# A hybrid transformer block on one core: the plan of all stages with TensorE's measured durations, a set duration for changes of its tile shape, and a small weight on a stage's age

## The chip, the core and the metric

One core of a Trainium2 chip runs the whole program: TensorE (PE, with its weight loads PEld), VectorE (DVE), ScalarE (ACT), GpSimd (POOL), SyncE (SP, which here only issues DMAs) and the core's 16 DMA engines. The metric is the device time in microseconds (us) of one execution, the median over runs. One further execution was taken by the hardware profiler, and all rows in this document come from it.

## The reference, cut to what matters

x has 8 batches of 512 tokens, width 128, in fp32. Four residual sublayers follow each other, each behind a layer norm:

```python
x = x + attn_a(layernorm(x))   # 16 heads, q and k of 8 + 32 features, softmax, v of 8, Wo, all with biases
x = x + ffn(layernorm(x))      # top-1 of 8 experts: silu(x W1 + b1) W2 + b2, hidden width 512, times the gate
x = x + attn_b(layernorm(x))   # differential: 16 heads, softmax(q1 k1) - lam * softmax(q2 k2), v of 16, W_proj
x = x + ffn(layernorm(x))      # the same experts and gate again
```

## The kernel before, in words

**Groups.** The attention work is cut into 96 groups of four heads of one batch. Groups 0 to 31 are attention a (four groups a batch), groups 32 to 95 attention b (eight groups a batch, four for each of the two softmaxes). The program counts 16 "batches" b: 0 to 7 in attention a, 8 to 15 in attention b. In this document *stage A* is the program up to group 31 and *stage B* the part from group 32 to the last group.

**What one group costs.** TensorE computes every score twice. `smax` (L1131) gives 16 pieces of 128 x 512, one for each of four query tiles and four heads; VectorE reduces each to row maxima in `rowmax` (L1479). The maxima are turned (`mrow`, L1137), copied by ScalarE and sent by DMA into an extra row of the stacked operand STK. `score` (L1152) then gives 16 transposed pieces with the maximum already subtracted; ScalarE takes the exponent (`expo`, L1355) into P, and `pv` (L1165, four times a group) multiplies by V. ScalarE copies the result (`ocopy`, L1362), TensorE turns it (`oturn`, L1173) and VectorE divides (`normal`).

**The rest.** For each batch there are the turned input (`hturn`, L1087), the feature tiles (`feat`, L1099: six a batch in stage A, four in stage B), the values (`vproj`, L1107 to L1115), the turned and projected output (`aturn` L1182, `oproj` L1193/L1199), the gate (`gturn`, `glogit`, `gplace`), and 92 expert blocks of 128 rows (`xturn` L1238, `up` L1246, `down` L1261). In stage B the features pass through GpSimd (`turned`, `b_lo`) and DMAs (`put`, `stack`) before a group can use them. The last 19 expert blocks run behind the last group.

**Three tile shapes.** In stage A `smax` and `score` use 120 or 121 rows of the array. In stage B they use 32 rows each, in the strip of their head j (rows 32j to 32j+31), so that up to four run side by side; these are called *row tiles* here. `pv` writes 32 columns each for four heads side by side (*column tiles*). Everything else uses the whole array. A *visit* is an unbroken run of row tiles, between two stages of another shape.

**PSUM.** Of the eight banks one is `pv`'s; the other seven go round among all other stages. `smax` may hold four, `score` three. `smax` and `score` ask for one bank or two neighbouring ones; VectorE and ScalarE read two banks with one instruction if they come as a pair.

**What sets the order.** All engines run in program order, and that order is written out by `schedule()` (L192), a list scheduler that plays the whole program at build time. `STAGES` holds an engine and a duration for each stage, `HOP` the time until another engine sees the end, `LANDS` that of a DMA. Every job asks for its next stage with a *rank*, its age in units of groups (`smax` of group g has g - 1.92, the feature tiles of a batch are spread over the groups before it is needed). The inner loop (L667) takes, over all engines, the request with the earliest start, and among equal starts the lowest rank:

```python
key = (start, rank)
if best is None or key < best[0]:
    best = (key, e, k)
```

For TensorE there is a `rows_free` time for each of the four row strips. In the plan of before a row tile in stage B occupies the engine for 0.03 us and its strip for 0.22, and a change of shape costs nothing by itself; the durations of the whole and column stages stand for what they take on average (`pv` 1.02, `up` 1.1, `gplace` 0.5).

Of the kernel before, what the change touches and what calls it, by code (L numbers as in the profile page):

```python
# [16 lines left out]
B = 8  # L17
# [142 lines left out]
def ends_of_segment(k):  # L160
# [3 lines left out]


STAGES = {
    "smax": ("tensor", 0.216), "score": ("tensor", 0.216), "pv": ("tensor", 1.02), "mrow": ("tensor", 0.11), "oturn": ("tensor", 0.45),
    "hturn": ("tensor", 0.45), "feat": ("tensor", 0.86), "vproj": ("tensor", 1.0), "aturn": ("tensor", 0.45), "oproj": ("tensor", 1.3), "gturn": ("tensor", 0.45), "glogit": ("tensor", 0.8),
    "gplace": ("tensor", 0.5), "xturn": ("tensor", 0.11), "up": ("tensor", 1.1), "down": ("tensor", 1.1),
    "rowmax": ("vector", 1.13), "normal": ("vector", 0.6), "join": ("gpsimd", 0.8), "split": ("gpsimd", 1.6), "ln_stats": ("vector", 1.3),  # L170
    "ln_apply": ("gpsimd", 2.4), "ln_apply_q": ("vector", 1.45), "columns": ("vector", 3.0), "flo": ("vector", 0.63),
    "resid": ("vector", 0.68),
# [5 lines left out]
    "gate_exp": ("scalar", 0.25), "silu_z": ("scalar", 0.48), "weigh": ("scalar", 0.2), "plus_p": ("gpsimd", 0.5), "mix": ("vector", 1.4), "wsum": ("tensor", 0.95), "silu_t": ("scalar", 0.49), "lambda_exp": ("scalar", 0.25),  # L178
    "index": ("gpsimd", 0.4), "ln_rstd": ("gpsimd", 0.6), "turned": ("gpsimd", 8.4), "silu_p": ("gpsimd", 2.8), "b_lo": ("gpsimd", 2.7), "scatter": ("gpsimd", 4.1), "send": ("gpsimd", 1.1),
    "xload": ("sync", 0.6), "setup": ("sync", 0.6), "put": ("sync", 1.8), "stack": ("sync", 1.2), "mput": ("sync", 0.6), "weights": ("sync", 1.1),  # L180
    "rows": ("sync", 1.1), "blank": ("sync", 0.6), "fill": ("sync", 9.0), "weights_b": ("sync", 0.6), "weights_p": ("sync", 0.6),
    "wload": ("sync", 1.0), "wstore": ("sync", 0.6),
}
HOP = {"tensor": 0.23, "vector": 0.13, "scalar": 0.14, "gpsimd": 0.15, "sync": 0.05}
LANDS = {"xload": 4.0, "setup": 3.0, "put": 3.0, "stack": 3.0, "mput": 2.0, "weights": 5.0, "rows": 3.8, "blank": 6.0, "weights_b": 4.0,
         "weights_p": 3.0, "wload": 14.0, "wstore": 8.0, "scatter": 4.0, "fill": 5.0, "send": 4.0}
FROM = [(19.77, 0.35), (33.0, 0.5), (74.0, 0.6), (100.00, 0.10)]

MAIN = ("smax", "rowmax", "score", "expo", "pv")
ENGINES = ("tensor", "vector", "scalar", "gpsimd", "sync")  # L190
# [2 lines left out]
def schedule(ticks=False):  # L193


    clock = {"tensor": 0.0, "vector": 3.5, "scalar": 3.0, "gpsimd": 5.0, "sync": 1.8}
    order = {e: [] for e in ENGINES}
    ended, ring, marks = {}, {}, []

    rows_free = [0.0] * 4  # L200
    idle = {bank: 0.0 for bank in RB}
    holder = {bank: None for bank in RB}
    asked, blocked = {e: [] for e in ENGINES}, {}
# [6 lines left out]
        yield from behind(stage, index)  # L210
        yield ("do", rank, stage, index, 0, us, engine)

    def fill_bank(rank, stage, *index):
        yield from behind(stage, index)
        yield ("do", rank, stage, index, 1, None, None)

    def fill_pair(rank, stage, *index):

# [13 lines left out]
    def find_banks(n, t, stage):  # L232

        kind = stage if stage in MOST else "other"
        held = sum(1 for bank in RB if bank not in idle and (holder[bank][0] if holder[bank][0] in MOST else "other") == kind)
        if held >= MOST[kind]:
            return None
        pair, single = free_banks(2) if n == 2 and held + 2 <= MOST[kind] else None, free_banks(1)
        if single is None:
            return None  # L240
        if n == 2 and held > 1 and kind == "smax":
            return pair
        return pair if pair and pair[0] <= max(t, single[0]) else single

    def rows_of(stage, index, n):
        if stage in ("smax", "score") and index[0] >= 4 * B:
            return range(index[-1] % 4, index[-1] % 4 + n)
        return range(4)
# [196 lines left out]
    def values_of(b, rank):  # L445
        if b in (0, 1, 2, B, B + 1, B + 2):
            if b >= 3:
                yield from after(("pv", (end_of(b - 3), 3)))
            yield from do(rank, "columns", b, us=3.0 if b < 3 else 0.4)
        if b >= 3:  # L450
            yield from after(("pv", (end_of(b - 3), 3)))
        if b == 0:
            yield from after(("setup", (3,)))
        for c in range(1 if b < B else 2):
            yield from fill_bank(rank, "vproj", b, c)
            yield from do(rank, "vcopy", b, c)
            give("vproj", b, c)

# [26 lines left out]
    def batch_ends():  # L485
        for b in range(NB):
            rank = first_of(b + 1) + (0.5 if closes(b) else 1.73)
# [6 lines left out]
                give("aturn", b, c)  # L494
            if b >= B:
                yield from after(("weights_p", ()))
            yield from fill_bank(rank, "oproj", b)
            yield from do(rank, "resid", b)
            give("oproj", b)
            rank += 0.2  # L500
# [23 lines left out]
            if closes(b):  # L524
                k = seg_of(b)
# [13 lines left out]
    def rank_of(m):  # L539
        k, i = BLOCKS[m]  # L540
        return FROM[k][0] + FROM[k][1] * i

# [125 lines left out]
    while any(asked.values()):  # L668
        best = None
        for e in ENGINES:  # L670
            for k, (rank, t, job, stage, index, bank, us) in enumerate(asked[e]):
                if bank:
                    found = find_banks(bank, max(t, clock[e]), stage)
                    if found is None:
                        continue
                    t = max(t, found[0])
                start = max(t, clock[e])
                if e == "tensor":
                    start = max([start] + [rows_free[r] for r in rows_of(stage, index, found[2] if bank else 1)])
                key = (start, rank)  # L680
                if best is None or key < best[0]:
                    best = (key, e, k)
        if best is None:
            raise RuntimeError("no stage can be placed")
        (start, _), e, k = best
        rank, t, job, stage, index, bank, us = asked[e].pop(k)
        if bank:
            _, first, n = find_banks(bank, max(t, clock[e]), stage)
            if stage in ("smax", "score"):
                us = n * (us if index[0] < 4 * B else 0.03)  # L690
            ring[stage, index] = [(b, holder[b]) for b in range(first, first + n)]
            for b in range(first, first + n):
                del idle[b]
                holder[b] = (stage, index)
        clock[e] = start + us
        more = 0.0
        if e == "tensor":
            taken = rows_of(stage, index, len(ring.get((stage, index), [0])))
# [5 lines left out]
        end = start + us + more + LANDS.get(stage, HOP[e])  # L704
# [1135 lines left out]
```

## Time and profile before

| | us |
|---|---|
| median of 3 runs | 1573.26 |
| lowest, highest | 1565.8, 1590.58 |
| the profiled execution: span | 1602.4 |
| PE busy over the span | 1416.2 (88%) |
| DVE busy | 1181.5 (74%) |
| ACT busy | 1080.7 (67%) |
| POOL busy | 693.2 (43%) |

No time outside the span is recorded for the profiled execution, so its span stands for its time: it is 29.1 us above the median of the three runs and 11.8 above the slowest. A busy share is a mean over stages with different limits, matmuls overlap, and their ends are modelled; how long PE was really held by one stage is read from the start of that stage to the start of the next. In the chain of waits each piece is what held up the next one; shares of the chain tell which engine came last.

### The profile page before, as it was taken

How to read it: one execution, taken by the hardware profiler on the slowest of the kernel's cores; microseconds unless marked ns; L12 is line 12 of the kernel's file. 1: busy time of each engine (PE TensorE's matmuls, PEld its weight loads, DVE VectorE, ACT ScalarE, POOL GpSimd, SP SyncE). 2: the span in 40 equal slices, each digit the busy share in tenths (PEclk: the TensorE clock that was granted, in tenths of full speed). 3: DMA queues.
4: the chain of work that ended last, by engine and by line, in shares of the span. 5: the costliest groups of instructions: out<-in, count | busy, mean ns of one | idle time of the engine just before them, and what ended most of it. 6: DMA issues, size and time to landing. Idle time of an engine off the chain costs nothing.

```text
span 1602.4 us, 26934 instructions
## 1 busy us (share of the span) xinstructions
PE 1416.2 (88%) x9196; PEld 597.4 (37%) x9196; DVE 1181.5 (74%) x2011; ACT 1080.7 (67%) x1787; POOL 693.2 (43%) x758
## 2 busy tenths in 40 slices
PE   3999999999999997889998899888888998998656
PEld 1334333345554332445433223222232544442245
DVE  4777788776767788647787887888787787779333
ACT  1566666766556776758786787787776886887612
POOL 3412334233414755666646581342511846552123
PEclk7999999999999999979999998999997998999868
DMA  6677676956742255978211220201205642411034
GB/s 189 187 232 229 187 237 175 264 164 194 210 117 77 78 177 165 300 206 231 84 30 40 61 60 21 80 27 41 57 24 187 194 120 91 132 39 34 1 123 136
DMA packets 131005, 208.46 MB, mean 130 GB/s; under 512 B 16611, under 2 KB 96128, under 8 KB 130870
## 3 DMA queue, kind: packets, MB, share of 16 engines
q1 hardware_dynamic: 121560, 192.40, 41.0%
q0 software_dynamic: 6016, 12.71, 2.3%
q10 hardware_dynamic: 3294, 1.64, 0.4%
q8 instruction: 74, 1.21, 0.3%
q14 instruction: 61, 0.50, 0.1%
HBM read 127.33 MB, written 80.77 MB: 130 GB/s over the span
## 4 chain that ended last, share of the span: by engine, by line
PE 65%; DVE 12%; ACT 6%; POOL 6%; issue 4%; DMA 4%; SPq 2%; ACTq 0%; another core or an unknown queue 0%; POOLq 0%; DVEq 0%
PE ps L1165 19%; PE ps L1131 12%; PE ps L1152 11%; DVE Mb L1479 7%; PE ps L1261 5%; PE ps L1246 5%; ACT P L1355 4%; PE ps L1099 4%; POOL ROW L1423 3%; PE ps L1173 2%; POOL rs L1701 1%; PE ps L1199 1%; PE ps L1218 1%; DVE st L1447 1%; DMA STK<-qka 1%
## 5 line engine op out<-in xcount | busy, mean ns | idle before, releaser
L1479 DVE TENSOR_REDUCE Mb<-ps 128x2 f32<-128x1024 f32 (+1 forms) x957 | 939.6, 1008 | 255.6 <-PE ps L1131 245.9
L1355 ACT ACTIVATE P<-ps 128x512 f32<-128x512 f32 (+1 forms) x1077 | 804.1, 780 | 250.4 <-PE ps L1152 232.0
L1131 PE MATMUL ps<-STK 32*128 32x512 f16 (+1 forms) x1536 | 418.1, 394 | 46.9 <-DMA STK<-qka 18.2
L1152 PE MATMUL ps<-STK 32*128 32x512 f16 (+1 forms) x1536 | 417.0, 392 | 40.9 <-ACT P L1355 25.0
L1165 PE MATMUL ps<-P,V 128*32 128x512 f32 x3072 | 425.7, 627 | 6.5 <-ACT P L1355 5.9
L1131 PEld LDWEIGHTS ps<-STK 32*128 32x128 f16 (+1 forms) x1536 | 103.1, 94 | 290.6 <-issue 109.4
L1152 PEld LDWEIGHTS ps<-STK 32*128 32x128 f16 (+1 forms) x1536 | 106.1, 93 | 268.9 <-issue 77.6
L1746 POOL DMA_INDIRECT xs<-ROW,slot x64 | 63.6, 993 | 136.3 <-DVE slot L1569 121.1
L1753 POOL TENSOR_TENSOR TH<-TH,Z 128x512 f32<-128x512 f32 x54 | 68.6, 1270 | 91.6 <-ACT Z L1403 91.1
L1165 PEld LDWEIGHTS ps<-P,V 128*32 128x32 f32 x3072 | 61.3, 109 | 124.4 <-issue 102.1
L1246 PE MATMUL ps<-XT,WE 128*128 128x128 f32 x696 | 102.3, 294 | 1.9 <-ACT XT L1385 1.1
L1246 PEld LDWEIGHTS ps<-XT,WE 128*128 128x128 f32 x696 | 89.4, 200 | 27.9 <-issue 13.4
L1710 POOL CAST HL<-RT 128x512 f16<-128x512 f32 x42 | 25.7, 613 | 151.2 <-ACT RT L1294 140.9
L1261 PEld LDWEIGHTS ps<-WE,Z 128*128 128x128 f32 x584 | 74.2, 199 | 36.4 <-issue 18.9
L1261 PE MATMUL ps<-WE,Z 128*128 128x128 f32 x584 | 86.0, 292 | 1.6 <-ACT P L1355 0.8
L1099 PE MATMUL ps<-HT,WA 128*128 128x512 f32 x160 | 86.2, 641 | 1.2 <-ACT HT L1280 0.8
L1768 POOL DMA_INDIRECT x<-X x46 | 46.4, 1009 | 81.4 <-DVE X L1651 65.6
L1699 POOL TENSOR_SCALAR vs<-mv 128x4 f32<-128x4 f32 x32 | 7.5, 234 | 167.2 <-DVE mv L1450 167.2
L1423 POOL TENSOR_SCALAR ROW<-ROW,mv,rs 128x128 f32<-128x128 f32 x100 | 78.4, 793 | 2.4
L1362 ACT COPY OR<-ps 128x512 f32<-128x512 f32 x96 | 56.4, 588 | 23.4 <-PE ps L1165 22.0
L1755 POOL TENSOR_TENSOR Z<-Z,TH 128x512 f32<-128x512 f32 x54 | 68.6, 1271 | 4.2
L1737 POOL TENSOR_TENSOR AT<-AT,OT 128x256 f32<-128x256 f32 x32 | 23.3, 728 | 108.4 <-DVE OT L1501 108.3
(156 smaller groups left out, 1407.0 us busy)
## 6 DMA issues: line engine op xcount, KB each, us to landing
WE<-wx SPq DMA_DIRECT2D x87, 576.0 KB
STK<-qka SPq DMA_DIRECT2D x62, 480.0 KB
qka<-HL SPq DMA_DIRECT2D x96, 256.0 KB
STK<-qkb SPq DMA_DIRECT2D x64, 256.0 KB
xs<-pad SPq DMA_DIRECT2D x8, 1554.0 KB
qkb<-HL SPq DMA_DIRECT2D x96, 128.0 KB
X<-xs SPq DMA_DIRECT2D x73, 129.5 KB, 3.7
qka<-HL SPq DMA_DIRECT2D x48, 128.0 KB
```

Of the source, the lines that this page charges most:

```text
L1099: eng.matmul(ps[:, bank, :], WA[:, 128 * x:128 * x + 128], HT[:, b % 2, :], start=True, stop=True).then_inc(sem("pr"), 1)
L1131: mm = eng.matmul(ps[:, bank + i, :], l_, r_, start=True, stop=True)
L1152: mm = eng.matmul(ps[:, bank + i, :], l_, r_, start=True, stop=True)
L1165: mm = eng.matmul(ps[32 * j:32 * j + 32, OB, :], V[:, b % 3, kt, vw * h:vw * h + 32], P[:, st % 3, j, :], start=(kt == 0), stop=(kt == 3))
L1246: mm = eng.matmul(ps[:, bank, 128 * c:128 * c + 128], w_[:, 128 * c:128 * c + 128], xt_, start=True, stop=True)
L1261: mm = eng.matmul(ps[:, bank, 0:128], z[:, 128 * c:128 * c + 128], w_[:, FH + D * c:FH + D * c + D], start=(c == 0), stop=(c == 3))
L1355: eng.activation(P[:, st % 3, j:j + n, :], ps[:, bank:bank + n, :], ACT.Exp, scale=SCALE_A if g < 4 * B else SCALE_B).then_inc(sem("exp"), 1)
L1423: eng.tensor_scalar(ROW[:, t0 + i, 0:128], ROW[:, t0 + i, 128:256], mv[:, z, i, 0:1], rs[:, z, i:i + 1], ALU.subtract, ALU.mult).then_inc( ...
L1479: eng.tensor_reduce(Mb[:, g % 2, at:at + 4 * n - 3:4], ps[:, bank:bank + n, :], AX, ALU.max).then_inc(sem("mx"), 1)
L1746: eng.indirect_dma_start(out=xs[k][:, :], out_offset=bass.IndirectOffsetOnAxis(ap=slot[:, t:t + 1], axis=0), in_=ROW[:, t, 0:ROWW], in_off ...
L1753: eng.tensor_tensor(th, th, z, ALU.mult).then_inc(sem("fq"), 1)
L1755: eng.tensor_tensor(z, z, th, ALU.add).then_inc(sem("fsp"), 1)
```

## The change

Nothing that is computed changes, and no instruction gets another shape except that a pair of pieces can become two singles and the reverse. The planner gets other numbers and two new rules:

- tensor durations: the middle lines of the diff, and `vproj` and `oproj` of stage B get durations of their own (0.87, 1.78);
- `TURN = 0.097`: a stage of another shape than the one before it starts at the earliest 0.097 after the work on all four strips has ended;
- a row tile holds its strip for its full 0.216 a piece, and the engine's own clock moves on by 0.01;
- `WEIGHT["tensor"] = 0.08`: among the requests on TensorE the one with the smallest start + 0.08 x rank is taken. Across the engines the earliest start still decides.

```diff
-    "smax": ("tensor", 0.216), "score": ("tensor", 0.216), "pv": ("tensor", 1.02), "mrow": ("tensor", 0.11), "oturn": ("tensor", 0.45),
+    "smax": ("tensor", 0.216), "score": ("tensor", 0.216), "pv": ("tensor", 0.88), "mrow": ("tensor", 0.11), "oturn": ("tensor", 0.44),
...
-    "gplace": ("tensor", 0.5), "xturn": ("tensor", 0.11), "up": ("tensor", 1.1), "down": ("tensor", 1.1),
+    "gplace": ("tensor", 0.21), "xturn": ("tensor", 0.11), "up": ("tensor", 0.89), "down": ("tensor", 0.89),
...
-HOP = {"tensor": 0.23, "vector": 0.13, "scalar": 0.14, "gpsimd": 0.15, "sync": 0.05}
+TURN = 0.097
+HOP = {"tensor": 0.21, "vector": 0.13, "scalar": 0.14, "gpsimd": 0.15, "sync": 0.05}
...
+WEIGHT = {"tensor": 0.08, "vector": 0.0, "scalar": 0.0, "gpsimd": 0.0, "sync": 0.0}
...
+    def shape_of(stage, index):
+
+        if stage in ("smax", "score") and index[0] >= 4 * B:
+            return "rows"
+        return "columns" if stage == "pv" else "whole"
...
                 if e == "tensor":
-                    start = max([start] + [rows_free[r] for r in rows_of(stage, index, found[2] if bank else 1)])
-                key = (start, rank)
-                if best is None or key < best[0]:
-                    best = (key, e, k)
+                    if shape_of(stage, index) == shape[0]:
+                        start = max([start] + [rows_free[r] for r in rows_of(stage, index, found[2] if bank else 1)])
+                    else:
+                        start = max([start] + [free + TURN for free in rows_free])
+                key = (start + WEIGHT[e] * rank, rank)
+                if mine is None or key < mine[0]:
+                    mine = (key, (start, rank), e, k)
+            if mine and (best is None or mine[1] < best[0]):
+                best = mine[1:]
...
-            if stage in ("smax", "score"):
-                us = n * (us if index[0] < 4 * B else 0.03)
+            if stage in ("smax", "score") and index[0] < 4 * B:
+                us = n * us
...
-            more = 0.19 if len(taken) < 4 else 0.0
-            for r in taken:
-                rows_free[r] = start + us + more
+            shape[0] = shape_of(stage, index)
+            for r in rows_of(stage, index, len(ring.get((stage, index), [0]))):
+                rows_free[r] = start + us
+            if shape[0] == "rows":
+                clock[e] = start + 0.01
```

Counted over TensorE's whole order, what the new plan does to it is this (a change of shape is a stage whose shape differs from that of the stage ahead of it):

| | before | after |
|---|---|---|
| changes of shape, stage A | 240 | 238 |
| changes of shape, stage B | 1077 | 915 |
| visits in stage B | 490 | 423 |
| `smax` pairs and singles, stage B | 374, 276 | 358, 308 |
| `score` pairs and singles, stage B | 284, 485 | 257, 540 |
| order of TensorE behind the last group | 64 stages | the same 64 |

**Place 1**, TensorE, in group 80, where experts run. Two `pv` (L1165, in the new file L1180) of one group and what stands ahead of each. L1131 and L1152 are `smax` and `score` (now L1146 and L1167), L1261 `down` (now L1276), L1246 `up` (now L1261). The array shape is not in these rows: all on STK are row tiles here. Before:

```order
L1131 MATMUL ps<-STK 128x512 x2
L1152 MATMUL ps<-STK 128x512
L1261 MATMUL ps<-WE,Z 128x128 x4
L1152 MATMUL ps<-STK 128x512 x2
L1131 MATMUL ps<-STK 128x512
L1165 MATMUL ps<-P,V 32x512 x4
L1131 MATMUL ps<-STK 128x512 x2
L1152 MATMUL ps<-STK 128x512 x2
L1246 MATMUL ps<-XT,WE 128x128 x4
L1131 MATMUL ps<-STK 128x512 x2
L1152 MATMUL ps<-STK 128x512 x2
L1165 MATMUL ps<-P,V 32x512 x4
```

The same group with the change (L1197 `aturn`, L1253 `xturn`, L1114 a feature tile of batch 15, L1214 `oproj`):

```order
L1146 MATMUL ps<-STK 128x512 x2
L1167 MATMUL ps<-STK 128x512
L1276 MATMUL ps<-WE,Z 128x128 x4
L1197 MATMUL ps<-idf,AT 128x128 x4
L1253 MATMUL ps<-idf,X 128x128
L1114 MATMUL ps<-HT,WA 128x512
L1214 MATMUL ps<-WA,ATT 128x128 x8
L1261 MATMUL ps<-XT,WE 128x128 x4
L1167 MATMUL ps<-STK 128x512 x2
L1146 MATMUL ps<-STK 128x512
L1180 MATMUL ps<-P,V 32x512 x4
```

Before, each whole stage stood alone between two visits; now six of them stand in one block, with one change of shape into it and one out of it.

**Place 2**, TensorE, in group 68, where no expert runs: one stretch between two `pv`. Before, with a feature tile of batch 15 (L1099) between two visits:

```order
L1165 MATMUL ps<-P,V 32x512 x4
L1131 MATMUL ps<-STK 128x512 x2
L1152 MATMUL ps<-STK 128x512 x2
L1099 MATMUL ps<-HT,WA 128x512
L1131 MATMUL ps<-STK 128x512 x2
L1152 MATMUL ps<-STK 128x512 x2
L1131 MATMUL ps<-STK 128x512 x2
L1165 MATMUL ps<-P,V 32x512 x4
```

The same stretch with the change:

```order
L1180 MATMUL ps<-P,V 32x512 x4
L1146 MATMUL ps<-STK 128x512 x2
L1167 MATMUL ps<-STK 128x512
L1146 MATMUL ps<-STK 128x512
L1167 MATMUL ps<-STK 128x512 x2
L1180 MATMUL ps<-P,V 32x512 x4
```

The feature tile has gone to a later place (batch 15's four tiles stood at groups 68 to 69 and stand at 73 to 80 now; those of batches 10, 12, 13 and 14 are moved and spread alike), and the visit holds six pieces where two visits held four and six.

## Rows read from the trace of the kernel before

**Rows 1.** Busy time by stage: engine, busy us (instructions), then PEclk, DMA share, GB/s.
```profile
37.00:555.00 518.00, 496.88 (x2861) 211.82 (x2861) 396.66 (x689) 333.53 (x500) 193.28 (x222) 1.00 0.63 184
555.00:1508.00 953.00, 855.84 (x5940) 332.06 (x5938) 737.21 (x1159) 721.39 (x1236) 461.19 (x475) 0.95 0.34 101
1508.00:1602.00 94.00, 53.37 (x376) 48.49 (x372) 33.38 (x109) 19.24 (x43) 24.86 (x26) 0.76 0.35 111
```

**Rows 2.** Chain of waits, 960 to 1230: share of that stretch by line.
```profile
by line: PE ps L1165 26.4%; DVE Mb L1479 12.0%; PE ps L1152 10.8%; PE ps L1131 9.8%; ACT P L1355 9.6%; issue 5.4%; POOL ROW L1423 4.6%; PE ps L1099 3.2%; PE ps L1173 2.8%; PE ps L1199 2.2%; PE ps L1115 2.0%; POOL rs L1701 1.5%; PE ps L1218 
```

**Rows 3.** Chain of waits, 1230 to 1508: share by line.
```profile
by line: PE ps L1165 26.0%; PE ps L1131 11.9%; PE ps L1152 10.8%; PE ps L1246 10.5%; ACT P L1355 10.0%; PE ps L1261 9.8%; DVE Mb L1479 3.9%; PE ps L1173 3.8%; issue 3.0%; DVE X L1638 2.1%; PE ps L1238 1.5%; PE ps L1199 1.4%; PE ps L1137 1.0
```

**Rows 4.** Waits, 555 to 1508: who for whom, us, times, longest.
```profile
DVE Mb L1479 <- PE ps L1131: 159.3, 212, 6.2
ACT P L1355 <- PE ps L1152: 122.6, 188, 3.2
```

**Rows 5.** Timeline of PE: start us, us to last modelled end, line, shapes, count.
```profile
1273.55 1.16 PE L1246 MATMUL ps<-XT,WE 128*128 128x128 f32 x8
1274.55 1.06 PE L1261 MATMUL ps<-WE,Z 128*128 128x128 f32 x8
1275.54 0.39 PE L1152 MATMUL ps<-STK 32*128 32x512 f16 x2
1275.55 0.39 PE L1131 MATMUL ps<-STK 32*128 32x512 f16 x1
1275.86 1.06 PE L1165 MATMUL ps<-P,V 128*32 128x512 f32 x8
...
1281.30 1.16 PE L1246 MATMUL ps<-XT,WE 128*128 128x128 f32 x8
1282.39 0.39 PE L1131 MATMUL ps<-STK 32*128 32x512 f16 x2
```

**Rows 6.** Chain of waits, 836 to 872: start us, us, what.
```profile
841.30 0.44 PE ps L1173 x4
...
852.28 1.86 PE ps L1165 x8
...
862.72 1.05 PE ps L1099 x2
...
864.09 1.00 PE ps L1165 x8
...
869.23 0.59 PE ps L1182 x4
```

**Rows 7.** Chain of waits, 0 to 90.
```profile
61.90 0.86 PE ps L1099 x2
```

**Rows 8.** Timeline of PE, 1084 to 1086: a visit of seven pieces.
```profile
1084.50 0.39 PE L1131 MATMUL ps<-STK 32*128 32x512 f16 x2
1084.51 0.60 PE L1152 MATMUL ps<-STK 32*128 32x512 f16 x4
1084.73 0.37 PE L1131 MATMUL ps<-STK 32*128 32x512 f16 x1
1085.98 0.66 PE L1173 MATMUL ps<-idf,OR 128*128 128x128 f32 x4 [0.88 <-ACT P L1355]
```

**Rows 9.** Groups by form, DVE, 555 to 1508: busy us, mean ns, idle before.
```profile
L1479 DVE TENSOR_REDUCE Mb<-ps 128x2 f32<-128x1024 f32 x375 | 452.2, 1220 | 129.3 <-PE ps L1131 124.4 <-remote 2.4 <-issue 0.6
L1479 DVE TENSOR_REDUCE Mb<-ps 128x1 f32<-128x512 f32 x276 | 184.3, 684 | 36.9 <-PE ps L1131 34.9 <-issue 0.3
```

**Rows 10.** Groups by form, ACT, 555 to 1508.
```profile
L1355 ACT ACTIVATE P<-ps 128x1024 f32<-128x1024 f32 x285 | 291.2, 1025 | 62.2 <-PE ps L1152 58.4 <-issue 0.8 <-ACT Mt L1333 0.6
L1355 ACT ACTIVATE P<-ps 128x512 f32<-128x512 f32 x485 | 277.7, 600 | 72.2 <-PE ps L1152 64.2 <-issue 3.8 <-remote 1.1
```

**Rows 11.** Windows, line L1165 alone: PE busy (matmuls), PEld busy, PEclk, DMA, GB/s.
```profile
1198.00:1226.00 28.00, 11.61 (x48) 1.21 (x48) 0.51 0.36 124
1226.00:1274.00 48.00, 12.79 (x96) 1.89 (x96) 1.00 0.73 223
```

More of the change, by code:

```diff
@@ L166 @@
 STAGES = {
-    "smax": ("tensor", 0.216), "score": ("tensor", 0.216), "pv": ("tensor", 1.02), "mrow": ("tensor", 0.11), "oturn": ("tensor", 0.45),
-    "hturn": ("tensor", 0.45), "feat": ("tensor", 0.86), "vproj": ("tensor", 1.0), "aturn": ("tensor", 0.45), "oproj": ("tensor", 1.3), "gturn": ("tensor", 0.45), "glogit": ("tensor", 0.8),
-    "gplace": ("tensor", 0.5), "xturn": ("tensor", 0.11), "up": ("tensor", 1.1), "down": ("tensor", 1.1),
+    "smax": ("tensor", 0.216), "score": ("tensor", 0.216), "pv": ("tensor", 0.88), "mrow": ("tensor", 0.11), "oturn": ("tensor", 0.44),
+    "hturn": ("tensor", 0.44), "feat": ("tensor", 0.86), "vproj": ("tensor", 1.1), "aturn": ("tensor", 0.44), "oproj": ("tensor", 1.1), "gturn": ("tensor", 0.44), "glogit": ("tensor", 0.92),
+    "gplace": ("tensor", 0.21), "xturn": ("tensor", 0.11), "up": ("tensor", 0.89), "down": ("tensor", 0.89),
     "rowmax": ("vector", 1.13), "normal": ("vector", 0.6), "join": ("gpsimd", 0.8), "split": ("gpsimd", 1.6), "ln_stats": ("vector", 1.3),
@@ L177 @@
     "vcopy": ("scalar", 0.5), "b_hi": ("scalar", 1.0), "acopy": ("scalar", 0.49), "gcopy": ("scalar", 0.49),
-    "gate_exp": ("scalar", 0.25), "silu_z": ("scalar", 0.48), "weigh": ("scalar", 0.2), "plus_p": ("gpsimd", 0.5), "mix": ("vector", 1.4), "wsum": ("tensor", 0.95), "silu_t": ("scalar", 0.49), "lambda_exp": ("scalar", 0.25),
+    "gate_exp": ("scalar", 0.25), "silu_z": ("scalar", 0.48), "weigh": ("scalar", 0.2), "plus_p": ("gpsimd", 0.5), "mix": ("vector", 1.4), "wsum": ("tensor", 0.86), "silu_t": ("scalar", 0.49), "lambda_exp": ("scalar", 0.25),
     "index": ("gpsimd", 0.4), "ln_rstd": ("gpsimd", 0.6), "turned": ("gpsimd", 8.4), "silu_p": ("gpsimd", 2.8), "b_lo": ("gpsimd", 2.7), "scatter": ("gpsimd", 4.1), "send": ("gpsimd", 1.1),
@@ L198, in schedule @@
     ended, ring, marks = {}, {}, []
-    rows_free = [0.0] * 4
+    rows_free, shape = [0.0] * 4, ["whole"]
     idle = {bank: 0.0 for bank in RB}
@@ L211, in do, with fill_bank @@
         yield ("do", rank, stage, index, 0, us, engine)
-    def fill_bank(rank, stage, *index):
+    def fill_bank(rank, stage, *index, us=None):
         yield from behind(stage, index)
-        yield ("do", rank, stage, index, 1, None, None)
+        yield ("do", rank, stage, index, 1, us, None)
     def fill_pair(rank, stage, *index):
@@ L454, in values_of @@
         for c in range(1 if b < B else 2):
-            yield from fill_bank(rank, "vproj", b, c)
+            yield from fill_bank(rank, "vproj", b, c, **({} if b < B else dict(us=0.87)))
             yield from do(rank, "vcopy", b, c)
@@ L496, in batch_ends @@
                 yield from after(("weights_p", ()))
-            yield from fill_bank(rank, "oproj", b)
+            yield from fill_bank(rank, "oproj", b, **({} if b < B else dict(us=1.78)))
             yield from do(rank, "resid", b)
@@ L670, in schedule @@
         for e in ENGINES:
+            mine = None
             for k, (rank, t, job, stage, index, bank, us) in enumerate(asked[e]):
@@ L694, in schedule @@
                 holder[b] = (stage, index)
-        clock[e] = start + us
-        more = 0.0
+        clock[e], hop = start + us, HOP[e]
         if e == "tensor":
-            taken = rows_of(stage, index, len(ring.get((stage, index), [0])))
-            more = 0.19 if len(taken) < 4 else 0.0
-            for r in taken:
-                rows_free[r] = start + us + more
+            shape[0] = shape_of(stage, index)
[3 more added lines that the diff above has]
+                clock[e] = start + 0.01
         order[e].append((stage, index))
         times[e].append((start, us, stage, index))
-        end = start + us + more + LANDS.get(stage, HOP[e])
+        end = start + us + LANDS.get(stage, hop)
         ended[stage, index] = end
```

## The prediction

> **What bounds the kernel now.** I read the busy time by stage first. In stage A TensorE is busy 496.88 of 518.00 us at full granted clock, in stage B 855.84 of 953.00 at a mean clock of 0.95, where VectorE has 737.21 (77%) and ScalarE 721.39 (76%) [rows 1]. Then the chain of waits: in the stretch without experts (960 to 1230) the lines of TensorE shown add up to 57.2%, with VectorE's reduce at 12.0% and the exponent at 9.6% [rows 2]; with experts (1230 to 1508) to 76.7%, the reduce at 3.9%, the exponent at 10.0% [rows 3]. The reader is to see that TensorE is what mostly comes last, and that stage B is not full on any engine: VectorE waited 159.3 us for `smax`, ScalarE 122.6 us for `score` [rows 4]. Seven PSUM banks go round between three engines, and whichever comes late hands its delay on. The 94 us behind the last group [rows 1] keep their order on TensorE.
>
> **The price of a change of shape.** I take starts. `up` at 1273.55 has row tiles before it and `down` behind it: 1.00 us to the next start. The `down`, with row tiles behind it: 0.99. The `up` at 1281.30 stands between row tiles on both sides: 1.09 [rows 5]. A feature tile among whole stages holds TensorE for 0.86 us [rows 7], between row tiles for 1.05 [rows 6]; four transposes for 0.44 and 0.59 [rows 6]. So one change costs 0.09 to 0.10 us; I use 0.10. The new TURN (0.097) is right, and durations without changes (0.86, 0.89, 0.44) are what the rows show once the changes are taken off. The Trainium skill, TensorEngine Tiling (Array Packing), Key Properties, says that changing the tiling mode drains TensorE, while changing only the tile does not. The trace agrees, with 0.10 us; the page has no price.
>
> **The sum, against the profiled 1602.4.**
>
> 1. Stage A: 240 changes become 238, the pieces are the same work, and an order on an engine that is busy 96% of the time cannot save more than its gaps, 21 us in all [rows 1]. I take 0, with 3 us either way.
> 2. Stage B, changes: 1077 - 915 = 162 fewer, 162 x 0.10 = 16.2 us less held by TensorE. TensorE is busy 90% of stage B [rows 1]; the chain gives it less, 57 to 77% [rows 2, 3]. An earlier end counts where TensorE is last, and I take the upper figure, because where it is not last the piece after next usually hangs on it again: 14.6. The lower end is 57%: 9.2.
> 3. Fuller visits: a visit with one piece a strip takes 0.32 us (1275.54 to 1275.86) [rows 5], and each further piece in the fullest strip about 0.22. Over all visits the pieces in the fullest strip add up to 714 before and 682 after: 32 x 0.22 = 7.0 us less at most. But a long visit waits for banks: the seven pieces from 1084.50 on took 1.48 us to the next start, 0.88 of it idle until the exponent gave a bank back [rows 8]. That row says that a longer visit saves nothing. I keep half, 3.5; ends 0 and 7.0.
> 4. Broken pairs: `smax` has 16 pairs fewer, `score` 27. Two singles cost VectorE 2 x 0.684 - 1.220 = 0.148 us more than a pair [rows 9], ScalarE 2 x 0.600 - 1.025 = 0.175 [rows 10]: 2.4 and 4.7 us. On the chain these two stand with some 4 to 12% and 10% each [rows 2, 3], but a single also gives its bank back earlier. I take 1.3 us of the 7.1; ends 0 and 7.1.
> 5. Long blocks. VectorE can hold four banks, two pairs, 2 x 1.22 = 2.44 us of work [rows 9]. If TensorE makes no visit for longer than that, VectorE must run dry, and ScalarE with its three banks earlier. With each stage at its duration without changes (0.90 for `pv`, that is 1.00 less one change; 0.86 for `feat`, 0.89 for `up` and `down`, 0.44 for four transposes, 0.11 for one, 0.87 for `vproj` and 1.78 for `oproj` as the new table has them) I find 2 such blocks in stage B before, 1.8 us over the limit together, and 21 after, 20.6 us over. Place 1 is the longest, 4.97 us. That is 18.8 us of new hunger on VectorE. Most of it falls where experts run, there the reduce is only 3.9% of the chain [rows 3] and VectorE has gaps to catch up in; I take a quarter, 4.7 us; ends 0 and 18.8.
> 6. Moved projections. The feature tiles of batches 10 and 12 to 15 come later, one every two groups instead of four close together. Their `put` stands at least two groups ahead of the first `stack` that wants it (batch 10: 42.25 against 44.75 in the new plan), and a group takes some 14 us (953 / 64 = 14.9), so the DMAs stay covered; if the cover of one batch went, its group would start late by up to a group's 15 us, once. POOL is busy 461.19 of 953 [rows 1] and takes batch 15's turning beside expert work. I take 0.
>
> Together: -14.6 - 3.5 + 1.3 + 4.7 = -12.1, so a like execution would span 1590.3. The change is taken as a number of us, since it stands on counts: 1573.3 - 12.1 = 1561.2. From the ends of the terms: -16.2 - 7.0 - 3 = -26 at one side, 1547; -9.2 + 7.1 + 18.8 + 3 = +20 at the other, 1593.
>
> **Rivals.**
>
> *More than the changes: the plan fits the chip.* The old plan gave `gplace` 0.5 us, where 0.21 stands now, and a row tile 0.03 us of the engine, and knew no change of shape, so its moments were wrong by tenths in each group. If the new order meets its partners on time, some of the 282 us that VectorE and ScalarE waited for TensorE [rows 4] goes, and spread feature tiles keep TensorE steadier where its clock fell. Half clock is dear: from 1198 to 1226 the granted clock was 0.51, the 1.2 GHz level, and six `pv` took 11.61 us busy there against twelve in 12.79 behind it [rows 11]; one held TensorE for 1.86 us instead of 1.00 [rows 6]. Six times 0.87 is 5.2 us, and I estimate another 4 for the visits around them: 9 of 28 us, a third. A mean clock of 0.95 means a tenth of stage B, 95 us, at half clock, which ties up some 31 us. If 15 of these came back and a tenth of half the waits, 14, the gain would be 12 + 15 + 14 = 41 us at best; half of the additions gives 1573.3 - 12.1 - 14.5 = 1547, the whole 1532. For it: every duration in the table is now what the rows show. Against: the waits are between engines that all work at 75% or more, and the old durations of `pv`, `up` and `down` already had the changes in them on average.
>
> *Evacuation sets the pace, and nothing comes of it.* The Trainium skill, TensorEngine Tiling (Array Packing), PSUM Bottleneck, warns that tiling speeds up TensorE and not the emptying of PSUM. As a mechanism here: what TensorE saves it spends waiting for a bank, as in the 0.88 us [rows 8], and the 3.5 and 14.6 are lost; left are the 1.3 of the singles: 1574.6. For it: VectorE and ScalarE wait on banks in the same ring, and the visits get longer. Against: these two themselves wait 282 us for TensorE, and TensorE's lines lead the chain [rows 2 to 4].
>
> *Long blocks starve the other two: slower.* The place is the stretches with experts and projections of stage B. The price is the whole 18.8 us of term 5 and the 7.1 of term 4. What gives it the decision is VectorE having no spare time to catch up in, that is from a busy share of it in those stretches near 90% on; then term 2 is worth its lower end: -9.2 + 18.8 + 7.1 = +17, 1590. If TensorE's clock then fell for half as long again in stage B, a further 15 us, 1605. For it: place 1 has 5 us without one row tile. Against: VectorE is at 77%, and experts also occupy TensorE longest.
>
> *The change does not do what it says* would be an order on the chip with other counts; the order is fixed in the program, so I give it no share.
>
> **How the numbers follow.** The forecast, 1561, has 0.5; the better fit, 1532 to 1547, 0.22; no gain, 1575, 0.18; slower, 1590 to 1605, 0.10. About 2% is what a measurement of this kernel can tell from no change: 1541.8 and 1604.7. Faster by over 2% is most of the better fit, half of its band and its tail, and a rest of the forecast: 0.20. Slower by over 2% needs the starving and the clock together: 0.04. Within 2%: 0.76. The range leaves out the far end of both: 1534 to 1588.
>
> **What would show it.** Right: stage A of the same length within 5 us; TensorE busy in stage B down by some 15 to 20 us with the same pieces; `up` and `down` in neighbouring pairs at 0.89 to 1.00; the exponent and reduce with a higher mean share of singles; waits of VectorE for `smax` about equal, with new single waits of 1 to 3 us behind blocks like place 1. Wrong: VectorE's waits for TensorE in stage B above 180 us (starving), or below 130 (fit); a mean granted clock in stage B away from 0.95 by more than 0.02; new waits of `smax` for `stack` DMAs near groups 48, 64, 72, 80 or 88 (term 6); stage A shorter by more than 5 us.

## The result, and the profile after

The changed kernel took 1561.86 us (median of 9 runs, 1554.73 to 1567.92) beside 1573.6 for the kernel before (also of 9): ratio 0.9922, 95% interval 0.9897 to 0.9948, or 12 us less. I had said 1561. In a second set of runs the ratio was 0.9839 (0.9773 to 0.9904). The size was right; how it comes about was in good part not what I wrote.

The profiled execution spans 1553.0 us. The one of before spanned 1602.4, more than any timed run of it, so the 49 us between them are not the change. I took a second profile of before (`before_again`), which spans 1586.0, and later one of the changed kernel (`after_again`), 1569.6: between the second profiles there are 16 us. By stage, the changed kernel (columns as in [rows 1]):

```profile
37.00:551.00 514.00, 497.02 (x2860) 212.83 (x2864) 393.72 (x696) 333.15 (x522) 192.04 (x220) 0.99 0.62 185
551.00:1462.00 911.00, 822.38 (x5943) 328.04 (x5940) 736.35 (x1176) 719.14 (x1264) 462.96 (x477) 0.98 0.36 106
1462.00:1553.00 91.00, 51.54 (x376) 46.99 (x372) 32.38 (x109) 19.91 (x43) 24.74 (x26) 0.75 0.35 114
```

and stage B of the second profile of before:

```profile
554.00:1491.00 937.00, 840.42 (x5944) 327.88 (x5940) 737.22 (x1159) 720.95 (x1237) 461.30 (x475) 0.97 0.35 103
```

Against the second profile of before, stage A is 3 us shorter, the tail 4, stage B 26 us at the same work of VectorE and ScalarE. TensorE is busy 18 us less in it, near the 16 counted, but only 9 less (831.77) in the changed kernel's second profile, whose stage B takes 926 us. The waits of the two, stage B of the changed kernel first, then of before, answer to [rows 4]:

```profile
DVE Mb L1494 <- PE ps L1146: 101.7, 146, 6.3
ACT P L1370 <- PE ps L1167: 79.5, 152, 2.0
```

```profile
DVE Mb L1479 <- PE ps L1131: 143.8, 209, 6.7
ACT P L1355 <- PE ps L1152: 116.2, 177, 3.2
```

79 us of waiting for TensorE have gone, and what is left of VectorE's, 101.7 (104.6 in the second profile), is below the 130 us that I had set as the sign of another cause. The other sign, a mean granted clock in stage B more than 0.02 from 0.95, is there in the first profile (0.98) and not in the second (0.97); the second profile of before has 0.97 as well. The place tells more. I cut stage B where the last `pv` of groups 31, 47, 71 and 95 starts: experts, none, experts. Columns as in [rows 1]. Before (second profile), then the changed kernel, then the last two stretches of the changed kernel's second profile:

```profile
583.00:845.00 262.00, 230.89 (x1673) 105.38 (x1670) 198.48 (x321) 195.37 (x345) 159.03 (x168) 0.96 0.60 177
845.00:1159.00 314.00, 279.21 (x1887) 86.20 (x1883) 261.04 (x403) 245.65 (x418) 148.83 (x148) 0.97 0.17 49
1159.00:1490.00 331.00, 301.10 (x2224) 126.39 (x2225) 256.61 (x398) 259.24 (x440) 138.41 (x146) 0.96 0.32 99
```

```profile
580.00:844.00 264.00, 235.88 (x1678) 110.77 (x1682) 196.09 (x328) 196.77 (x358) 174.57 (x180) 0.95 0.59 175
844.00:1131.00 287.00, 256.76 (x1851) 80.37 (x1843) 256.86 (x397) 234.42 (x398) 108.55 (x114) 0.99 0.18 50
1131.00:1461.00 330.00, 301.46 (x2245) 128.50 (x2245) 258.90 (x407) 267.56 (x481) 167.82 (x170) 0.99 0.33 102
```

```profile
852.00:1145.00 293.00, 259.83 (x1851) 81.33 (x1847) 257.04 (x397) 234.70 (x397) 110.52 (x116) 0.98 0.17 50
1145.00:1477.00 332.00, 303.24 (x2245) 128.63 (x2245) 259.09 (x407) 267.73 (x481) 167.75 (x170) 0.98 0.33 101
```

The middle, where no expert runs, is shorter: 314 to 287 and 293 us, with VectorE busy 83% of it before (261.04 of 314) and 89% after (256.86 of 287; the 97 to 99% of my expectation below is a misreading of these rows). The two stretches with experts, where 67 and 52 of the changes of shape are saved, take as long as before.

But the stretches no longer hold the same work. Counted in TensorE's order, the middle had 20 feature tiles, 4 turned inputs and 8 value stages, and has 12, 3 and 6 now. The stretch ahead of it went from 4 feature tiles to 8, the one behind from none to 5, with one turned input and two value stages more. GpSimd's busy time moved along: 148.83 to 108.55 in the middle, 138.41 to 167.82 behind it. At the durations without changes the moved stages are 8 x 0.86 + 0.44 + 2 x 0.87 = 9 us of TensorE (an estimate), and the middle has 47 changes of shape fewer. So a good part of the 21 to 33 us is work that now lies elsewhere, and the stretches with experts took it in without growing. The sum of the three stretches is the fairer measure: 923 and 907 us before, 881 and 891 with the change.

### The profile page after: what moved, and what is told of

It reads as the page before. It is cut to its first block, busy times and chain, and to the rows that moved or that the text cites. A ratio compares the mean times of both kernels' runs of the same rounds, so it can differ in the third digit from the quotient of the medians.

```text
span 1553.0 us, 27030 instructions
## 1 busy us (share of the span) xinstructions
PE 1380.2 (89%) x9196; PEld 592.6 (38%) x9196; DVE 1176.7 (76%) x2034; ACT 1078.8 (69%) x1837; POOL 693.6 (45%) x758
## 4 chain that ended last, share of the span: by engine, by line
PE 61%; DVE 10%; ACT 9%; POOL 6%; DMA 6%; issue 6%; SPq 2%; ACTq 0%; POOLq 0%; DVEq 0%
PE ps L1180 18%; PE ps L1146 11%; PE ps L1167 10%; ACT P L1370 6%; DVE Mb L1494 6%; PE ps L1261 4%; PE ps L1276 4%; PE ps L1114 4%; POOL ROW L1438 3%; PE ps L1188 2%; DMA X<-xs 2%; PE ps L1214 1%; POOL rs L1716 1%; DMA STK<-qka 1%; PE ps L1233 1%
## 5 line engine op out<-in xcount | busy, mean ns | idle before, releaser
L1146 PE MATMUL ps<-STK 32*128 32x512 f16 (+1 forms) x1536 | 410.8, 388 | 44.5 <-DMA STK<-qka 18.5
L1167 PE MATMUL ps<-STK 32*128 32x512 f16 (+1 forms) x1536 | 412.3, 386 | 29.9 <-ACT P L1370 20.3
L1180 PE MATMUL ps<-P,V 128*32 128x512 f32 x3072 | 414.5, 612 | 7.7 <-ACT P L1370 6.4
L1146 PEld LDWEIGHTS ps<-STK 32*128 32x128 f16 (+1 forms) x1536 | 105.2, 94 | 297.5 <-DVE Mb L1494 107.1
L1167 PEld LDWEIGHTS ps<-STK 32*128 32x128 f16 (+1 forms) x1536 | 108.1, 93 | 258.2 <-ACT P L1370 86.3
L1180 PEld LDWEIGHTS ps<-P,V 128*32 128x32 f32 x3072 | 60.7, 108 | 122.7 <-issue 102.2
L1261 PE MATMUL ps<-XT,WE 128*128 128x128 f32 x696 | 98.4, 286 | 3.5 <-issue 1.9
L1261 PEld LDWEIGHTS ps<-XT,WE 128*128 128x128 f32 x696 | 87.6, 196 | 21.4 <-issue 11.0
L1276 PE MATMUL ps<-WE,Z 128*128 128x128 f32 x584 | 83.3, 286 | 3.3 <-POOL Z L1770 1.4
L1114 PE MATMUL ps<-HT,WA 128*128 128x512 f32 x160 | 85.0, 630 | 1.3 <-ACT HT L1295 1.2
L1276 PEld LDWEIGHTS ps<-WE,Z 128*128 128x128 f32 x584 | 72.3, 193 | 32.2 <-issue 10.6
L1733 POOL TENSOR_TENSOR RT<-RT,CS 128x512 f32<-128x512 f32 x32 | 40.6, 1278 | 65.8 <-ACT RT L1318 65.7
L1377 ACT COPY OR<-ps 128x512 f32<-128x512 f32 x96 | 56.6, 590 | 18.8 <-PE ps L1180 17.5
```

Source lines behind the costliest of these rows:

```text
L1114: eng.matmul(ps[:, bank, :], WA[:, 128 * x:128 * x + 128], HT[:, b % 2, :], start=True, stop=True).then_inc(sem("pr"), 1)
L1146: mm = eng.matmul(ps[:, bank + i, :], l_, r_, start=True, stop=True)
L1167: mm = eng.matmul(ps[:, bank + i, :], l_, r_, start=True, stop=True)
L1180: mm = eng.matmul(ps[32 * j:32 * j + 32, OB, :], V[:, b % 3, kt, vw * h:vw * h + 32], P[:, st % 3, j, :], start=(kt == 0), stop=(kt == 3))
L1261: mm = eng.matmul(ps[:, bank, 128 * c:128 * c + 128], w_[:, 128 * c:128 * c + 128], xt_, start=True, stop=True)
L1276: mm = eng.matmul(ps[:, bank, 0:128], z[:, 128 * c:128 * c + 128], w_[:, FH + D * c:FH + D * c + D], start=(c == 0), stop=(c == 3))
```

## The experiments

Three sets of runs on two chips; the kernel before took 1592, 1589 and 1577 us in them. Ratios are to before in the same set. The table has the counts from TensorE's order in stage B (changes of shape; us by which long blocks exceed 2.44), the ratio, the three stretches of the profile in us with their sum, and the mean granted clock, averaged over the executions that the ratio rests on, the kernel's and those of before.

| kernel | changes | over | ratio, 95% interval | 31-47 | 47-71 | 71-95 | sum | clock, that of before |
|---|---|---|---|---|---|---|---|---|
| before, both profiles | 1077 | 1.8 | 1 | 268, 262 | 320, 314 | 335, 331 | 923, 907 | |
| changed, both profiles | 915 | 20.6 | 0.992, 0.984 | 264, 266 | 287, 293 | 330, 332 | 881, 891 | 0.960, 0.956 (second set) |
| `turn_zero` | 1098 | 2.6 | 1.0065 (1.003-1.010) | 278 | 304 | 360 | 942 | 0.945, 0.953 |
| `turn_double` | 755 | 54.9 | 1.0068 (1.004-1.010) | 271 | 299 | 341 | 911 | 0.951, 0.953 |
| `no_weight` | 864 | 43.2 | 1.036 (1.031-1.041) | 301 | 301 | 352 | 954 | 0.931, 0.953 |
| `weight_only` | 1097 | 0.6 | 0.983 (0.977-0.989) | 271 | 289 | 341 | 901 | 0.960, 0.956 |
| `more_changes` | 1239 | 20.6 | 1.001 (0.996-1.005) | 271 | 301 | 333 | 905 | 0.954, 0.956 |
| `more_tiles` | 915 | 20.6 | 0.985 (0.978-0.991) | 266 | 292 | 333 | 891 | 0.961, 0.956 |
| `weight_feats` | 1097 | 1.5 | 0.994 (0.991-0.996) | 262 | 290 | 340 | 892 | 0.961, 0.961 |
| `weight_rest` | 1043 | 13.6 | 1.052 (1.046-1.058) | 274 | 339 | 339 | 952 | 0.939, 0.961 |
| `late_feats_before` | 1100 | 2.1 | 0.996 (0.992-1.000) | 259 | 302 | 333 | 894 | 0.958, 0.961 |
| `late_feats_after` | 913 | 27.1 | 0.990 (0.986-0.994) | 265 | 290 | 339 | 894 | 0.963, 0.961 |

The last column is there because the time follows TensorE's granted clock. Of 29 executions of before in the first of these sets, one at a mean of 0.962 took 1580.6 us and one at 0.939 took 1604.07; a line through all of them gives 11 us for each 0.01 (an estimate). By that rate some 9 of `turn_zero`'s 11 us, 24 of `no_weight`'s 58 and 24 of `weight_rest`'s 85 go with a lower clock, and 4 or 5 of the 17 to 19 that `weight_only` and the changed kernel gained go with a higher one; of `weight_feats`' 10 us none do. Whether an order lowers the clock, or loses time and clock by one cause, no run shows.

**Before again.**

> The kernel before, unchanged, for a second profile of it. The profiled execution of before spanned 1602.4 us with a mean granted clock of 0.948, above all its timed runs; the changed kernel's spanned 1553.0 with 0.965. If that gap of 49 us is the change's, this profile spans about 1600 with 100 us of stage B at half clock again; if most of it was that one execution, it spans 1565 to 1580 and shows less half clock. The time itself should be 1.000 of before.

Span 1586.0, ratio 0.999, 61 us of stage B at half clock instead of 102. So 16 of the 49 us between the first two profiles were that execution. Another 17 were the changed kernel's, whose second profile spans 1569.6 against 1553.0.

**TURN and the weight, one at a time.** In the changed kernel:

```diff
-TURN = 0.097
+TURN = 0.0        # turn_zero; 0.2 in turn_double
```

> The changed kernel with TURN = 0: new durations and the weight on age stay, a change of shape is free in the plan. The order then has 1098 changes of shape in stage B (before 1077, changed kernel 915) and 8 long blocks. Theory C (the gain is the fewer changes, 0.10 us each, nine tenths of it kept): 21 more than before is +2 us, more pieces in the fullest strip (751 against 714) +4, ratio to before 1.00 to 1.005. Rival F (the gain is the better fit of the other durations and the weight): most of the gain stays, ratio 0.99 to 0.995. Rival N (any new order moves the time by some us, without a law): anything within 0.99 to 1.01.

> The changed kernel with TURN = 0.2, twice what a change costs on the chip: 755 changes of shape in stage B (162 + 160 fewer than before), but 47 long blocks without a row tile with 54.9 us beyond VectorE's 2.44 (changed kernel: 21 and 20.6; before 2 and 1.8). Theory C with my quarter for the hunger: -322 x 0.09 = -29, longer visits -7, broken pairs +2, long blocks +13: -21 us, ratio 0.987. Theory S (long blocks starve VectorE at their whole price): -29 - 7 + 2 + 53 = +19, ratio 1.012. Rival F (fit): a wrong duration again, ratio back towards 1.00.

1603.3 and 1604.9 us. With TURN at zero the gain is lost, a little more than theory C says. With TURN doubled there are 160 changes fewer than in the changed kernel, worth 12 to 16 us, and it takes some 1.5 to 2.3% longer than that one: nearer theory S than theory C. If the long blocks are the cause, 34 us more of them cost about their whole price or above it. They were not varied alone: the order also has more singles, and some 10 us of the difference go with a lower clock (0.951 against 0.960). VectorE waited 123.9 us for `smax` in stage B, about 20 more than in the two profiles of the changed kernel, in 107 waits instead of 146 and 147: fewer and longer ones, as starving would have it.

```diff
-WEIGHT = {"tensor": 0.08, ...}
+WEIGHT = {"tensor": 0.0, ...}
```

> The changed kernel with a weight of 0 on age: 864 changes of shape in stage B, 34 long blocks, 43.2 us beyond 2.44. Theory C: -213 x 0.09 = -19, longer visits -3, broken pairs +2, long blocks a quarter of 41 = +10: -10 us, ratio 0.993, the same as with the weight. Theory S: +20, ratio 1.013. Rival W (the weight brings the gain): ratio near 1.00, and single long waits for stages that came late.

1650.1 us, the largest effect of all, beyond what any theory had. The fewer changes of shape are there (864) and do not help. Something in the weight carries the kernel.

**A second profile of the changed kernel, and the weight alone** on the kernel before:

```diff
-                key = (start, rank)
+                key = (start + WEIGHT[e] * rank, rank)
...                                             # the best of each engine first, then the earliest start, as in the change
```

> The changed kernel, unchanged, for a second profile on one chip with the runs below. Ratio 0.992 as measured. In its first profile groups 47 to 71 took 288 us against 314 to 319 in the two profiles of before, with VectorE busy 97 to 99% there; if that is the kernel's and not that execution's, it stands here again within 4 us.

> The kernel before with nothing but the weight of 0.08 on age on TensorE: old durations, no TURN. Its order has 1097 changes of shape in stage B (before 1077) and 3 long blocks, and the feature tiles of batches 10 and 12 to 15 are spread out as in the changed kernel. Theory C (fewer changes are the gain): 20 x 0.09 = +2 us, longer visits +2, ratio 1.00 to 1.004. Theory W (the weight is the gain, as the 57 us lost without it suggest): ratio 0.99 or below, and groups 47 to 71 shorter than 314 us by 10 or more. If both parts are needed together (without the weight the planner with TURN puts off what is old), ratio 1.00 and the changed kernel stays ahead of it by its 0.8%.

1570.5 and 1572.0 us. The weight alone, with 20 changes *more* than before, gives as much as the whole change in the same set (0.983 and 0.984, intervals of 0.6% either way), with 289 us in groups 47 to 71, where it has 13 feature tiles instead of 20. Theory C falls as the account of the gain.

**Does a change of shape cost anything, then?** In the changed kernel's own order:

```diff
...                                             # extra: 162 smax pieces of stage B that follow another row tile
+                if (g, c) in extra:
+                    eng.matmul(ps[:, bank, 0:8], ones[:, :], ones[:, 0:8], start=True, stop=True)
```

> The changed kernel in its own order, with 162 small matmuls of the whole array (8 columns, overwritten by the piece behind them) put into visits of stage B, each in front of an smax piece that follows another row tile: 324 changes of shape more, 32 us held on TensorE and some 0.03 us each for the matmul itself, 5 us. Theory C as forecast (nine tenths of what TensorE is relieved of or loaded with shows): +29 to +33 us, ratio to before about 1.012. Theory V (where VectorE is full, groups 47 to 71, and where the ring of banks decides, TensorE's time is partly free): half of it or less, +10 to +16 us, ratio about 1.00.

> The control to the run with 324 changes more: the same 162 places, the small matmul as a row tile in the strip of the piece behind it, so no change of shape. Both theories: +0 to +5 us on the changed kernel, ratio to before 0.992 to 0.995. If it costs as much as the run with changes, the changes are not what that run shows.

1594.1 us with 324 changes more, 1570.5 with the same matmuls as row tiles. 23.5 us for 324 changes is 0.073 us each; the intervals of the two ratios leave some 10 to 45 us, and about 7 of the 23.5 go with a lower clock (0.954 against 0.960). Theory C's mechanism holds, about three quarters of the 0.10 us show. 162 changes fewer are then worth some 12 us, which something takes back.

**What the weight does.** It puts off what is young: above all the feature tiles, asked for up to 20 groups ahead. In before they were computed as soon as TensorE had a gap, and then lay in PSUM. Of batch 14's four in `before_again`, TensorE (first view) and ScalarE's copy (second):

```profile
1022.77 1.12 PE L1099 MATMUL ps<-HT,WA 128*128 128x512 f32 x2
1028.63 1.13 PE L1099 MATMUL ps<-HT,WA 128*128 128x512 f32 x2
1031.33 1.12 PE L1099 MATMUL ps<-HT,WA 128*128 128x512 f32 x2
1037.38 1.02 PE L1099 MATMUL ps<-HT,WA 128*128 128x512 f32 x2
```

```profile
1023.93 0.58 ACT L1303 COPY RT<-ps 128x512 f32<-128x512 f32 x1 [0.23 <-PE ps L1099]
1029.92 0.59 ACT L1303 COPY RT<-ps 128x512 f32<-128x512 f32 x1
1044.98 1.07 ACT L1303 COPY RT<-ps 128x512 f32<-128x512 f32 x2
```

The third tile is done at 1032.5 and copied at 1045.0: its buffer RT is in GpSimd's hands until shortly before (`turned`, `b_lo` of the pair before end at 1043.8). For 12 us one of seven banks is out of the ring, and for the last 7 of them the fourth tile's as well. From start of the tile to start of the copy, summed over the 32 tiles of stage B (this pair among them), it is 215 us in `before_again`, 119 of them in batches 12 to 15, and 119 and 19 in `after_again`, 305 and 186 in `no_weight`. This time is called *holds* below.

> The kernel before with the weight of 0.08 on the age of the turned input, the feature tiles and the values alone; every other stage on TensorE is weighed as if its rank were the current group. 1097 changes of shape, 6 long blocks; the feature tiles stand where the weight on all stages puts them. Theory H (what the weight brings is that a feature tile no longer holds one of the seven banks: in the trace of before the 32 feature tiles of stage B wait 215 us in their banks for ScalarE's copy, 119 of them in batches 12 to 15, with the weight on all stages 108 and 29): ratio 0.985 as with the weight on all, groups 47 to 71 near 290 us. Rival O (what counts is that old stages such as score and pv go first): ratio 1.00, groups 47 to 71 near 315.

> The complement: the weight on all stages of TensorE but the turned input, the feature tiles and the values. 1043 changes of shape, 15 long blocks, the feature tiles stand early and close together as before. Theory H: no gain, ratio 1.00, groups 47 to 71 near 315 us, feature tiles hold their banks for 200 us or more. Rival O: ratio 0.985 or so.

```diff
-                key = (start + WEIGHT[e] * rank, rank)
+                key = (start + WEIGHT[e] * (rank if stage in ("hturn", "feat", "vproj") else now_at), rank)
...                                             # the rest as in weight_only; now_at counts the groups whose pv stand
```

1567.1 us, and 290 in groups 47 to 71, with 12 feature tiles in them. The weight on these three stages alone makes the kernel 0.4 to 0.9% faster at an unchanged clock; that placing the projections later gains time is shown. The complement (`not in`) took 1662.1: holds 372 us, middle 339, of which 75 us at half clock (before 29 and 18). It is no clean complement: with rank replaced by the current group the feature tiles are preferred to all that is younger than it, and stage A lost some 35 us too. The three stretches of `weight_rest`, and then of `weight_feats`:

```profile
617.00:891.00 274.00, 240.96 (x1684) 110.92 (x1680) 200.86 (x314) 194.92 (x347) 163.08 (x171) 0.93 0.56 166
891.00:1230.00 339.00, 297.18 (x1865) 86.95 (x1857) 259.60 (x411) 246.07 (x423) 140.99 (x140) 0.89 0.16 45
1230.00:1569.00 339.00, 304.84 (x2223) 127.93 (x2220) 257.10 (x397) 260.79 (x446) 138.05 (x146) 0.96 0.32 97
```

```profile
577.00:839.00 262.00, 236.06 (x1681) 107.37 (x1680) 200.09 (x312) 198.49 (x346) 168.98 (x174) 0.93 0.60 175
839.00:1129.00 290.00, 261.74 (x1860) 80.43 (x1863) 257.91 (x407) 236.76 (x400) 113.28 (x118) 1.00 0.17 50
1129.00:1469.00 340.00, 315.97 (x2246) 129.74 (x2249) 260.07 (x400) 267.70 (x464) 167.49 (x170) 0.95 0.32 99
```

**The bank alone.** One line in the plan, no weight:

```diff
+        if b >= B and n >= NA * B + 2:
+            yield from after(("b_lo", ((n - NA * B) // 2 - 1,)))
         yield from fill_bank(rank, "feat", n)
```

> The kernel before, no weight and no TURN, with one line more in the plan: in stage B the first tile of a pair of feature tiles is asked for only when the buffer that its copy writes is free again (after b_lo of the pair before). The pairs of one batch still stand close together (batch 15: groups 69 to 71), but none waits long in a bank. 1100 changes of shape. Theory H: most of the weight's gain, ratio 0.985 to 0.99, groups 47 to 71 at 290 to 300 us, holds near 60 us. Rival Sp (the gain is the spreading of the projections' work over ScalarE and GpSimd, not the bank): ratio 1.00, groups 47 to 71 above 305 us.

> The changed kernel with the same line. The changed kernel's feature tiles hold banks for 119 us, 100 of them in batches 8 to 11, near the first groups of stage B. 913 changes of shape, 27 long blocks. Theory H: some 60 us less of one bank in seven in groups 27 to 50, worth 2 to 6 us at the rate of before (some 100 to 180 us less held went with 25 us): ratio 0.980 to 0.983, a little ahead of the changed kernel. Rival: there VectorE waits for DMAs and experts, not for banks, and nothing changes: ratio 0.984.

The first kernel's three stretches:

```profile
576.00:835.00 259.00, 231.65 (x1679) 106.12 (x1682) 199.03 (x328) 196.43 (x353) 166.46 (x175) 0.97 0.61 179
835.00:1137.00 302.00, 271.94 (x1873) 82.34 (x1871) 260.17 (x394) 241.49 (x411) 139.84 (x139) 0.98 0.17 51
1137.00:1470.00 333.00, 304.83 (x2221) 126.37 (x2221) 257.30 (x402) 262.26 (x455) 140.70 (x149) 0.96 0.32 99
```

In before: holds 43 us, middle 302, ratio 0.996, which the interval does not quite tell from 1. The middle still has 18 feature tiles here, against 12 in `weight_feats`, and what it lacks there it has back behind it (333 against 340). Over the three stretches the two take 894 and 892 us, and their ratios, 0.996 and 0.994, are not told apart. So keeping the banks free may be the whole of what `weight_feats` gains, or less of it; how much the spreading of the projections' work (which also sits on ScalarE and GpSimd) adds is not shown. Against holds as the one cause stands `no_weight`: with 305 us of them its middle takes 301 us, less than before's 314. It has 12 feature tiles and 47 changes of shape fewer there too. On top of the change the same line gave 1559.6 us, ratio 0.990: not told from the changed kernel. No version here clearly beats it.

## Why the prediction was right in size, and where its steps failed

1. *Stage A: 0, 3 us either way.* Right: 555 and 554 us before, 551 and 552 after. But the 94 us behind the last group were put at nothing for a wrong reason. They hold the same 64 stages, yet not in the same order: 16 of them (`up`, `down` and `xturn`) stand some places earlier or later. The new durations make that order: `weight_only`, on the old ones, has the order of before. From the start of the last `pv` to the end it was 95.0 and 96.2 us before and 96.1 in `weight_only`, 92.0 and 92.2 in the changed kernel and 92.3, 92.4 and 92.3 in `turn_zero`, `turn_double` and `no_weight`: some 3 or 4 us of the gain. In the last set the two orders are less far apart: 93.3, 94.1 and 98.6 for kernels with the old one, 93.7 for `late_feats_after`.
2. *Term 2, 162 changes at 0.10, nine tenths kept: -14.6.* The price holds; what shows is nearer three quarters, -12, by `more_changes`. But I took it for the whole gain; `weight_only` has the gain without it.
3. *Terms 3 and 4, fuller visits -3.5 and broken pairs +1.3.* Not tested apart. The table of orders counted two groups of stage A in: `score` of stage B has 277 pairs and 470 singles before, 247 and 530 after, so it breaks 30 pairs, not 27; that is 0.5 us.
4. *Term 5, long blocks, a quarter of 18.8: +4.7.* Mis-sized, as far as `turn_double` can say: it puts them at about the full price. Place 1 on the chip, VectorE:

```profile
1263.06 1.23 DVE L1494 TENSOR_REDUCE Mb<-ps 128x2 f32<-128x1024 f32 x1 [0.41 <-PE ps L1146]
1264.20 0.34 DVE L1653 SCALAR_TENSOR_TENSOR X<-WE,X 128x128 f32<-128x128 f32 x1
1267.37 0.69 DVE L1523 TENSOR_TENSOR ROW<-ROW,ps 128x512 f32<-128x512 f32 x1 [2.83 <-PE ps L1214]
```

   TensorE made no visit from 1262.95 to 1268.16, and VectorE stood for 2.83 us, ScalarE for 2.13. With 18.8 whole and -12 for the changes, terms 2 to 5 sum to about +5, not -12: the new durations and the rules on shape together add nothing that shows here, as `weight_only` against the changed kernel says (0.983, 0.984, each good to 0.6%).
5. *Term 6, moved projections: 0.* This was the step that failed. I asked only whether the tiles still came in time, not what they held while early. Placing them later gains 10 us by itself (`weight_feats`, 0.991 to 0.996); `weight_only`, which moves them almost alike, gained 17. What the middle shows, 21 to 33 us, is partly work moved out of it, and groups 71 to 95 pay for it: 340 and 341 us in `weight_feats` and `weight_only` against 331. There the changed kernel, with 72 and 71 changes fewer than these two, has 330 and 332. That, read from single profiles, is where I see TURN's use.

So two errors of opposite sign, a gain put at nothing and a cost put at a quarter, made the sum right: that is luck. The rival *the plan fits the chip* had the sign that I named (waits below 130 us) and the wrong main cause: with the new durations and no weight, or no TURN, the kernel is slower than before. It did name the spread feature tiles, for the clock's sake. In the middle 29 and 18 us stood at half clock before, 7 and 14 in the changed kernel, 3 in `weight_only`, none in `weight_feats`; at the prediction's third of such time that is between 1 and 10 us. *Long blocks starve* has its mechanism in place 1 and in the longer waits of `turn_double`; in the changed kernel its price is covered. *Evacuation sets the pace* has come nearer in the middle, where VectorE is now busy 89%. Term 6's fear, a missed DMA, did not come.

What stays open: why `turn_zero` is no faster than before, though it has the weight, 13 feature tiles in the middle and holds of only 121 us (29 us more than before in groups 71 to 95, where it has 22 changes of shape more and 68 us at half clock against 24); why `no_weight` lost 37 us in groups 31 to 47 (its profile has a single wait of 8.6 us for expert rows there, I did not test it), how far one reordering differs from another by chance, and the gap between `weight_only` (0.983) and `weight_feats` (0.994), measured on different chips.

## What to carry to other kernels

When a stage is moved, ask what it holds from start to release, not only whether it is in time: a result computed early in PSUM takes a bank out of a ring that everyone waits on. A greedy planner that takes the earliest start fills a gap with whatever can start, however young; a small weight on age, on the old durations and without any rule on shape, gave as much here as the whole change. A rule that saves changes of tile shape must be priced with the hunger that it may make for the engines that empty the banks: with twice the true price the kernel was slower than with no such rule at all (`weight_only`), though with a price of zero on the new durations (`turn_zero`) it was slower too. And before a gain is put down to a stretch of a profile, count the work in that stretch on both sides.

## What was not expected of the hardware

The same program's profiles differed by 16 us (1602.4 and 1586.0), with 102 and 61 us of stage B at the 1.2 GHz level; near 1200, where [rows 11] has 27 us at that level, the second profile has 14. And 162 small row-tile matmuls inside visits cost nothing that shows (1570.49 against 1570.51 us), while the same as whole-array matmuls cost 23.5.
